# Four perceptron products moved into the end of the attention before it, and an output product of two batches split into two

## The reference

```python
x = x + _L0_attn_ref(_layernorm(x), ...)    # "future" attention on a normed h, then a GELU perceptron on it
x = x + _L0_xattn_ref(_layernorm(x), ...)   # attention on an external context, with memory keys
x = x + _L0_ffn_ref(_layernorm(x), ...)     # mixture of 8 experts, top 2, and a shared one
x = x + _L1_attn_ref(_layernorm(x), ...)    # attention over offsets, gated
x = x + _L1_xattn_ref(_layernorm(x), ...)   # causal attention on the context
x = x + _L1_ffn_ref(_layernorm(x), ...)     # quantised gated perceptron
```

```python
h = layernorm(y, ln2_g, ln2_b)
y + gelu(h @ W_ff1) @ W_ff2        # 256 -> 1024 -> 256
```

## Time and profile before

| what | us |
|---|---|
| median of 3 runs | 1761.31 |
| lowest and highest run | 1760.13, 1769.48 |
| the profiled execution, whole | 1771.22 |
| its span, first to last instruction | 1769.4 |
| TensorE busy in the span | 1600.8 |
| DVE busy | 876.1 |
| ACT busy | 833.7 |
| POOL busy | 338.7 |
| mean granted clock of TensorE | 0.949 |

### The profile page before, as it was taken

One profiled execution on the slowest core, in us unless ns is written; L12 is line 12 of the kernel. 1 busy time (PEld: TensorE's weight loads), 2 busy tenths in 40 slices (PEclk: granted clock), 3 DMA queues, 4 the chain that ended last, 5 costly groups with the idle time before them and its releaser, 6 DMA issues. The chain is left out here.

```text
span 1769.4 us, 34614 instructions
## 1 busy us (share of the span) xinstructions
PE 1600.8 (90%) x13646; PEld 1039.5 (59%) x13646; DVE 876.1 (50%) x1828; ACT 833.7 (47%) x1712; POOL 338.7 (19%) x305
## 2 busy tenths in 40 slices
PE   8899999799799999999799999997887988799965
PEld 3355555455356665666556999995454665466642
DVE  4566766411555655655232111111655765377748
ACT  4355656433145544455331222223366877256656
POOL 0012121221100000101058000004504544112112
PEclk9999999899899999999699999999998999799978
DMA  7000000100200000000152999993586331000001
GB/s 256 1 1 1 1 1 1 32 22 1 83 19 20 20 12 18 20 11 3 56 195 87 323 327 327 323 327 114 138 200 164 91 75 37 21 12 12 1 1 42
DMA packets 148051, 150.16 MB, mean 85 GB/s; under 512 B 69890, under 2 KB 135106, under 8 KB 147890
## 3 DMA queue, kind: packets, MB, share of 16 engines
q1 hardware_dynamic: 144818, 140.60, 25.9%
q0 software_dynamic: 3072, 7.34, 1.3%
HBM read 120.40 MB, written 27.53 MB: 84 GB/s over the span
## 5 line engine op out<-in xcount | busy, mean ns | idle before, releaser
L945 DVE CUSTOM_DVE_ANT_0 x_unused<-psum,masked 112x439 f32<-112x439 f32 x256 | 142.0, 612 | 20.1 <-PE psum L768 19.2
L2370 DVE TENSOR_TENSOR masked<-masked 128x512 f32<-128x512 f32 x70 | 49.8, 711 | 200.9 <-ACT masked L2272 200.9
L883 ACT ACTIVATE x_probs<-psum,key_mask 125x448 f32<-125x448 f32 x192 | 106.2, 636 | 76.0 <-PE psum L788 76.0
L2213 PEld LDWEIGHTS psum<-mix_xb,mix_up 128*128 128x128 f32 x1120 | 130.6, 192 | 2.1 <-issue 0.4
L2213 PE MATMUL psum<-mix_xb,mix_up 128*128 128x128 f32 x1120 | 130.7, 275 | 0.0
L2223 PE MATMUL psum<-mix_down,masked 128*128 128x256 f32 x560 | 127.0, 380 | 0.1
L1444 PE MATMUL psum<-fold_full,hT 128*112 128x512 f32 x256 | 113.8, 597 | 1.3 <-DVE fold_part L1765 1.3
L2223 PEld LDWEIGHTS psum<-mix_down,masked 128*128 128x128 f32 x560 | 103.6, 190 | 13.3 <-DVE masked L2370 0.4
L768 PE MATMUL psum<-x_kT,x_qz 32*112 32x439 f32 x512 | 89.0, 595 | 3.2 <-DVE x_kT L930 3.2
L2272 ACT ACTIVATE masked<-psum 128x512 f32<-128x512 f32 x70 | 41.9, 598 | 97.0 <-PE psum L2213 97.0
L788 PE MATMUL psum<-x_qmax,x_kT 32*125 32x112 f32 (+1 forms) x2048 | 80.6, 284 | 4.6 <-DVE x_qmax L953 3.8
(11 more groups left out here) (328 smaller groups left out, 3308.9 us busy)
## 6 DMA issues: line engine op xcount, KB each, us to landing
mix_up<-in_moe_up SPq DMA_DIRECT2D x35, 1024.0 KB
mix_down<-in_moe_down SPq DMA_DIRECT2D x35, 1024.0 KB
offset_rows<-join_rows SPq DMA_DIRECT2D x16, 784.0 KB, 6.2
hrow<-offset_rows SPq DMA_DIRECT2D x16, 784.0 KB, 5.1
x_ctx<-in_ctxT SPq DMA_DIRECT2D x16, 375.0 KB, 3.1
slots_x<-masked SPq DMA_DIRECT2D x1, 4480.0 KB, 21.3
mix_rows<-slots_x SPq DMA_DIRECT2D x35, 128.0 KB, 3.4
slots_y<-mix_result SPq DMA_DIRECT2D x35, 128.0 KB, 3.6
```

Source lines behind the costliest of these rows:

```text
L883: nc.scalar.activation(probs[0:rows, 4 * (c % 2) + r], psum[0:rows, bank("tile", n, 4 * c + r), 0:G].rearrange("p (k t) -> p k t", k=4), A ...
L945: nc.vector.tensor_tensor_reduce(unused[:, at], psum[0:T, at, 0:KEYS], masked[0:T, n * KEYS:(n + 1) * KEYS], -1.0, -3.0 * NEG, ALU.add, AL ...
L2213: mm = nc.tensor.matmul(psum[:, 2 * u + half, m * BLOCK:(m + 1) * BLOCK], e_up[:, w, c, (half * H4 + m) * P:(half * H4 + m + 1) * P], xb[: ...
L2370: nc.vector.tensor_tensor(e_hidden[:, u, half * H4:(half + 1) * H4], e_relu[:, half], e_relu[:, half], ALU.mult).then_inc(hidden_ready.sem, 1)
```

## The change

**Products ahead.** A new constant `UPS_AHEAD = 4`. The future attention gets the perceptron's weights and a new semaphore `ups_ahead`. At the end of steps 15 and 16, before the output product, TensorE makes two up products of group 0 in each, m = 0 and 1, then 2 and 3, in the banks 0 to 3, after DVE's subtraction of batch 15 has read the bank. The perceptron begins group 0 with m = 4, and ACT's first four Gelus wait for `ups_ahead`. The Gelu table of group 0 is loaded in step 16 of the future attention, behind the norm's Ln and Exp.

**The last two outputs.** In the future and the causal attention, `output_of_last` makes the outputs of batches 14 and 15 one by one in steps 16 and 17, in banks 4 and 5, with one addition each. In step 16, ACT's copy, Ln and Exp of batch 15 stand before the norm's Ln and Exp of group 2, and DVE's spread of batch 15 before the norm's scale. In step 17 none of this is left.

**Semaphores.** The mixture's scope now has `reuse=True`.

```diff
 def gelu_perceptron(..., mask_keys, ups_ahead):
@@ tensor
             for x in (up_ready, hidden_read):
                 x.start(pe)
+            pe.sem_inc(up_ready.sem, UPS_AHEAD)
...
-                for m in range(M8):
+                for m in range(UPS_AHEAD if g == 0 else 0, M8):
                     pe.wait_ge(*act_done.after(n if m >= 4 else n - 1, (m - 4) % M8))
@@ scalar
-                nc.scalar.preload_act_table(ACT.Gelu)
+                if g:
+                    nc.scalar.preload_act_table(ACT.Gelu)
                 for m in range(M8):
-                    act.wait_ge(*up_ready.after(n, m))
+                    if g == 0 and m < UPS_AHEAD:
+                        act.wait_ge(ups_ahead, m + 1)
+                    else:
+                        act.wait_ge(*up_ready.after(n, m))
 def token_attention(..., perceptron=None, ups_ahead=None):
@@ tensor
+            def output_of_last(n):
+                bank = 4 + n % 2
+                pe.wait_ge(*normed.after(At(n)))
+                for m in range(C):
+                    for g in range(NG):
+                        mm = nc.tensor.matmul(psum[:, bank, m * T:(m + 1) * T], wt["wo"][:, g, m * P:(m + 1) * P], out_mixT[:, n % NM, g * T:(g + 1) * T], start=g == 0, stop=g == NG - 1)
+                mm.then_inc(projected.sem, 1)
+
+            def up_ahead(m):
+                if m == 0:
+                    perceptron.wait(pe)
+                    pe.wait_ge(*beside.behind.ready(0))
+                pe.wait_ge(*shifted.after(At(NB - 1), m))
+                for c in range(C):
+                    mm = nc.tensor.matmul(psum[:, m, 0:G], perceptron.at["up"][:, c, m * P:(m + 1) * P], hT[:, c, 0:G], start=c == 0, stop=c == C - 1)
+                mm.then_inc(ups_ahead, 1)
...
-                if not offset and n >= 3 and n % 2:
+                if future and n in (NB - 1, NB):
+                    for m in range(2):
+                        up_ahead(2 * (n - (NB - 1)) + m)
+                if not offset and n >= NB:
+                    output_of_last(n - 2)
+                elif not offset and n >= 3 and n % 2:
                     output_of_two(n - 3)
@@ scalar
-                if last:
+                if last and (offset or n <= NB):
                     take_logs(n - 2)
...
-                if last:
+                if last and (offset or n <= NB):
                     invert(n - 2)
+                if n == NB and not offset:
+                    copy_mix(n - 1)
+                    take_logs(n - 1)
+                    invert(n - 1)
                 beside.act_invert(act, n, 6)
+                if n == NB and future:
+                    nc.scalar.preload_act_table(ACT.Gelu)
...
-                if before:
+                if before and (offset or n < NB):
                     copy_mix(n - 1)
@@ vector
+            def add_of_last(n):
+                bank = 4 + n % 2
+                dve.wait_ge(*projected.after(At(NB // 2 - 1), n - (NB - 2)))
...
-                else:
+                elif n == NB:
                     spread_denominators(n - 2)
+                    spread_denominators(n - 1)
...
-                if not offset and n >= 3 and n % 2:
+                if not offset and n < NB and n >= 3 and n % 2:
                     add_two(n - 3)
                 beside.dve_scale(dve, n)
+                if not offset and n >= NB:
+                    add_of_last(n - 2)
@@ mixture
-    with Scope(nc, "mix") as s:
+    with Scope(nc, "mix", reuse=True) as s:
```

More of the change, by code:

```diff
@@ L560, in copy_even, with gelu_perceptron @@
             self.nc.vector.tensor_copy(*self.place(t)).then_inc(self.read_even, 1)
-def gelu_perceptron(nc, psum, w, hT, accT, yT, beside, next_weights, load_flags, mask_keys):
+UPS_AHEAD = 4
+def gelu_perceptron(nc, psum, w, hT, accT, yT, beside, next_weights, load_flags, mask_keys, ups_ahead):
     up, down = w.at["up"], w.at["down"]
@@ L1314, in _, with token_attention @@
                     take_queries(*QUERIES_AT_BATCH[n])
-def token_attention(nc, kind, stage, psum, const, w, hT, accT, beside, ready, next_weights, ctxT=None, qz_all=None, gateT=None, skewed=None, startup=None, folded=None, big=None, spare=None, room=None, stored=None):
+def token_attention(nc, kind, stage, psum, const, w, hT, accT, beside, ready, next_weights, ctxT=None, qz_all=None, gateT=None, skewed=None, startup=None, folded=None, big=None, spare=None, room=None, stored=None, perceptron=None, ups_ahead=None):
     future, offset, causal = kind == "future", kind == "offset", kind == "causal"
@@ L1816, in add_output @@
                 a.then_inc(added.sem, 1)
+            def add_of_last(n):
+                bank = 4 + n % 2
+                dve.wait_ge(*projected.after(At(NB // 2 - 1), n - (NB - 2)))
+                if future:
+                    x = accT[:, :, n * T:(n + 1) * T]
+                    nc.vector.tensor_tensor(x, x, psum[:, bank, 0:C * T].rearrange("p (c t) -> p c t", c=C), ALU.add).then_inc(added.sem, 1)
+                    return
+                for c in range(C):
+                    x = accT[:, c, n * T:(n + 1) * T]
+                    a = nc.vector.scalar_tensor_tensor(x, psum[:, bank, c * T:(c + 1) * T], wt["bo"][:, c:c + 1], x, ALU.add, ALU.add)
+                a.then_inc(added.sem, 1)
             def add_two(n):
@@ L2894, in start_act @@
                 first.act(act, affine_loaded)
+            ups_ahead = nc.alloc_semaphore("perceptron_ups_ahead")
             n2 = norm(yT, hT, ln2)
@@ L2899, in decoder @@
             token_attention(nc, "future", "a0", psum, const, a0, hT, yT, Beside(None, n2), first.ready_after, None, folded=folded,
-                            startup={"sp": start_sp, "dve": start_dve, "pe": start_pe, "act": start_act}, big=big, spare=masked[:].bitcast(F32))
+                            startup={"sp": start_sp, "dve": start_dve, "pe": start_pe, "act": start_act}, big=big, spare=masked[:].bitcast(F32), perceptron=f0, ups_ahead=ups_ahead)
             flags_loaded = Chain(nc.alloc_semaphore("flags_loaded"))
@@ L2917, in mask_keys @@
                 nc.vector.tensor_scalar(keys[:, :, 0:S2], flags[:].bitcast(U8).rearrange("p (b s) -> p b s", b=NB)[:, some], NEG, None, ALU.mult)
-            gelu_perceptron(nc, psum, f0, hT, xT, yT, Beside(n2, n3), x0, load_flags, mask_keys)
+            gelu_perceptron(nc, psum, f0, hT, xT, yT, Beside(n2, n3), x0, load_flags, mask_keys, ups_ahead)
         memory_attention(nc, psum, const, x0, hT, xT, a["ctxT"], Beside(n3, n4), shared)
```

## The result

| what | before | changed |
|---|---|---|
| median, us | 1762.68 (4 runs) | 1742.89 (4 runs) |
| lowest and highest, us | 1760.13, 1769.48 | 1740.14, 1745.91 |
| span of the profiled execution, us | 1769.4 | 1743.1 |
| TensorE busy, us | 1600.8 | 1586.6 |
| mean granted clock | 0.949 | 0.961 |

The ratio is 0.9884, with a 95% interval of 0.9858 to 0.9909. Two later comparisons of the same two kernels gave 0.9904 (0.9872 to 0.9936) and 0.9913 (0.9897 to 0.9929). The mean of the three ratios is 0.990, 17.6 us of 1762. The forecast was 1743.0 us, 18.3 us less than the median shown then. In the two later comparisons the medians of the changed kernel were 1748.65 and 1748.43 us, 13.8 and 15.2 us under the kernel before.

A forecast was written before the change was run, and what follows sets the result against it. TensorE, busy 90% of the span, was taken as the bound, with idle time and half-clock work to win. Gains of 7.0, 5.55 and 5.7 us, together 18.3, off the 1761.31 us median gave 1743.0 us; range 1737 to 1754.

The forecast's parts named there:

- Step n=15: Future attention: two up products fill TensorE's wait, so the output of batches 12 and 13 runs at full clock; 1.1 us gained.
- the hole: TensorE's 2.37 us wait in future attention step 15, before the output of 12 and 13; the clock falls with it.
- Step n=16 and the attention's end: Future attention: two products, single outputs at full clock and an earlier chain end it at 341.1 instead of 348.10, 7.0 us.
- The chain: Batch 15's copy, spread, Ln, Exp and POOL multiply, future attention step 16: run ahead of the norm, 1.2 us early.
- The table: Gelu table load in future attention step 16: its 1.28 us hidden under the output products.
- The perceptron's start: Four products of group 0 removed, 6.0 us, less 0.45 us later TensorE start behind the first Gelu; net 5.55 us.
- The causal end: Causal attention's end: single outputs and earlier chain finish at 1694.3 instead of 1700.03, 5.7 us; 1.8 less if the clock falls.
- What costs nothing: Clearing 27 semaphores on POOL in the offset attention, about 1.9 us, fits into 3.92 us of waiting.
- (a): At the outputs and perceptron's start the clock does not stay up: 8.9 us lost, gain 9.4, 1751.9 us; chance 0.15.
- (b): Perceptron's start: table or first Gelu late, TensorE waits 1.3 to 1.5 us more, 1744.5 us; chance 0.06.
- (c): Behind the joints the gain is given back as clock falls move in later gaps, 1752.4 us or more; chance 0.06.
- (d): Clock fallen at 323 stays low well into the perceptron: slower by 0.8 to 5.9 us, up to 1767.2; chance 0.04.

The follow-up runs named there:

- no_products_ahead: Changed kernel without the four products ahead, Gelu table loaded in the perceptron again; split outputs and advanced chain stay: 1742.25 us against 1755.46, ratio 0.9925.
- norm_first: Changed kernel with the norm's work queued before batch 15's chain again, outputs still one by one: future attention's end 20.47 us, causal end 9.08 us.
- filler_in_15: Kernel before with two extra products, results unread, in step 15's TensorE gap: 1756.08 us against 1755.46, ratio 0.9998.
- changed_third: Changed kernel run a third time without any edit, against the kernel before: 1748.43 us, ratio 0.9913.
- no_products_again: Second profile of the changed kernel without the products ahead: future attention's end 17.71 us, causal end 8.40 us.
- four_in_16: Changed kernel with all four products ahead in step 16 and none in step 15: 1753.95 us against 1762.47, ratio 0.9946.

## Why the prediction was right

The terms of the sum are borne out one by one at the joints. That the total came within 0.1 us of the forecast is luck: the median of the kernel before moved by 1.4 us with its fourth run, the first comparison has a gain of 19.8 us by the medians where the sum has 18.3, and the changed kernel's later medians lie 5.4 to 5.7 us above the forecast, inside its range.

**Step n=15** (-1.1 us): from batch 14's last mixes to batch 15's it is 10.61 us instead of 11.72, -1.11. The price is right, its reason only in part. The falls behind the hole were taken as certain; two of five profiles with the hole had none. In an execution without one the two products would cost 0.3 us there (10.28 in no_products_ahead) instead of gaining 1.1.

**Step n=16 and the attention's end** (7.0 us, the 1.1 of step 15 included): measured 7.11. The chain was early, at 333.77 against 335.0 for the second half of the last outputs, 1.2 us as worked out. The kernel norm_first shows that the slack was used: without the advanced chain 1.6 us are lost. The table was hidden; its load ended at 334.99, 2.25 us ahead of the last add's end.

**The perceptron's start** (5.55 us): measured 5.50. TensorE began 1.39 us after the add, I had 1.3.

**The causal end** (5.7 us): 5.91 in the first profile, 5.0 with a fall of the clock in one of three (and the same in one of the two profiles without the products, 8.40 us), a case that I had priced at 1.8 and that cost half.

**What costs nothing**: the semaphores. POOL in the changed kernel at the offset attention's start, and DVE ahead of it:

```profile
1324.76 1.15 DVE L1782 SCALAR_TENSOR_TENSOR second_result<-hrow,psum 112x448 f32<-112x448 f32 x2 [13.06 <-DMA hrow<-offset_rows]
...
1326.00 1.44 POOL L1970 TENSOR_TENSOR second_result<-second_result,weights 112x448 f32<-112x448 f32 x1 [5.55 <-DVE second_result L1782]
```

POOL waits 5.55 us for DVE here, more than in the earlier trace rows, where it was 3.92; what it waits for is DVE's multiplication, and that waits for the rows' transfer (filler_in_15, where the scope isn't handed on, has 5.03 us of the same wait). The trace has the 27 clearings themselves, from 1315.9 to 1317.8: 1.9 us as worked out, beside POOL's filling of a tile and its multiplications of weights, which run from 1315.89 to 1320.44, and nobody waits for them.

**The missing term**: the quantised block's start. The sum let the gap there stand as it was. The average and the variance run at full clock behind the new end, and d is about 1.3 us shorter (0.9 in the first pair). What keeps the clock up isn't shown: in changed_third and no_products_again the output of batch 14 ran at half clock, and the average and the variance were at full clock even so.

**The rivals.** (a), the clock that doesn't stay up, came true in pieces: half of c's price in changed_third, 1.7 us in b in four_in_16 and norm_first, never the whole 8.9. The three ratios of the changed kernel range over 5 us; of this the joints show 0.9, the fall in c. (b) was measured at 1.0 us, not 1.3 to 1.5. (c) can't be excluded in a small size: the four distances together are 18.5 to 19.9 us shorter in the changed kernel's three profiles than in the mean of the two before, and by their ratios the three comparisons have 20.4, 16.9 and 15.3 us, each with an interval of about 3 to 6 us on either side. In the profiles the stretches outside the joints differ in both directions. (d) didn't occur; the longest half clock at the first joint was that of the kernel before.

**The split of the gain** is what the sum did not say. It reads as if the products brought 5.55 us and more. Alone they bring 7.9 us at the joint and on top of the split only 4.2, since both work on the same hole: 8.4 + 7.9 is 3.7 us more than the 12.6 that they have together. About 1.4 of these 3.7 are step 15's clock, which stayed up in both profiles without the products for a reason that is open.

## What to carry to other kernels

At the end of a pipelined stage, look at the order of the engines that normalise the last item: work for the next stage that is queued ahead of it stands on the path there (1.6 us at each of two joints here). Fill the idle time of TensorE with the next stage's first products only after this, and count what both together leave, for they share the same hole. And before a chain is moved ahead of other work, list the buffers which that other work frees: in a third attention TensorE waited 1.81 us for a bank that was read late, and most of the expected gain didn't come.

## What the runs showed of the hardware

**A gap doesn't always cost the clock.** The same wait of 2.37 us ahead of the same product was followed by a fall in three profiles (4.97, 4.98 and 4.98 us for the output) and by none in two (3.29 us both). The gap of 1.8 to 2.8 us between the blocks was followed by one in two of nine profiles, at 1.7 us each, both behind a gap of 1.78. One kernel can show both outcomes: the end of the causal attention took 7.52, 7.52 and 8.43 us in the three profiles of the changed kernel, and 7.52 and 8.40 in the two without the products. The Trainium skill (TensorE: Matmul & The Clock Gate, section What's actually happening) says that the number of slow matmuls of one kernel varies from run to run; the causal end agrees with that (7.52 and 8.43 us), and for the hole in step 15 no run here shows two outcomes of one kernel.

**Chips differ in one stage.** From POOL's first gather of the experts' rows to its first instruction of the offset attention it took 106.0 to 106.9 us in the four profiles that were taken together on one chip and 115.5 to 117.8 us in all others, whatever the kernel. The medians of the kernel before, 1755.46 against 1762.5 to 1763.6 us, follow it. A comparison across chips would have shown 7 us that no edit made.
